# The last batch's Square in two halves about two means, joined by small GpSimd operations

## The reference

```
h   = gelu(x @ W_down[role] + b_down[role])      # 1024 -> 512
u   = h @ W_up[role] + b_up[role]                # 512 -> 1024
y   = x + u
mean = mean(y);  var = mean((y - mean)^2)        # over the 1024 values
out = (y - mean) / sqrt(var + 1e-5) * gamma[role] + beta[role]
```

## Time and profile before

| | us |
|---|---|
| median of 3 runs | 1415.9 |
| lowest, highest | 1415.86, 1416.5 |
| the profiled execution, its own time | 1416.17 |
| its span in the trace | 1414.7 |
| TensorE matmul busy | 1404.9 |
| VectorE busy | 1205.1 |
| ScalarE busy | 776.6 |
| GpSimd busy | 209.8 |

### The profile page before, as it was taken

One profiled execution on the slowest core, in us unless ns is written; L12 is line 12 of the kernel. 1 busy time (PEld: TensorE's weight loads), 2 busy tenths in 40 slices (PEclk: granted clock), 3 DMA queues, 4 the chain that ended last, 5 costly groups with the idle time before them and its releaser, 6 DMA issues.

```text
span 1414.7 us, 29421 instructions
## 1 busy us (share of the span) xinstructions
PE 1404.9 (99%) x6205; PEld 1163.1 (82%) x6206; DVE 1205.1 (85%) x1460; ACT 776.6 (55%) x2049; POOL 209.8 (15%) x312
## 2 busy tenths in 40 slices
PE   9999999999999999999999999999999999999997
PEld 8888888888888888888888888888888888888886
DVE  8798988888888888888899988888888888888887
ACT  5555555555555555555555555555555555555555
POOL 5376411100000000000476311100000000000000
PEclk9999999999999999999999999999999999999999
DMA  9678877766666556666778677766665666666664
GB/s 236 185 228 238 220 205 202 206 207 187 185 198 202 186 185 201 198 187 185 227 233 232 206 213 194 220 188 197 202 187 185 199 200 187 185 196 198 192 187 148
DMA packets 208998, 283.57 MB, mean 200 GB/s; under 512 B 25898, under 2 KB 155691, under 8 KB 208976
## 3 DMA queue, kind: packets, MB, share of 16 engines
q1 hardware_dynamic: 201006, 269.06, 62.5%
q0 software_dynamic: 6016, 12.15, 4.7%
q10 hardware_dynamic: 1954, 2.12, 0.6%
HBM read 183.35 MB, written 99.88 MB: 200 GB/s over the span
## 4 chain that ended last, share of the span: by engine, by line
PE 99%; DVE 1%; issue 0%; DVEq 0%; POOL 0%; POOLq 0%
PE p_up L1168 16%; PE p_up L1170 16%; PE p_up L1169 16%; PE p_down L1168 16%; PE p_down L1170 16%; PE p_down L1169 16%; PE p_down L1144 1%; PE p_down L1216 0%; PE p_down L1211 0%; PE p_down L1222 0%; PE p_up L1211 0%; PE p_up L1222 0%; PE p_up L1216 0%; PE p_hT L1164 0%; DVE row L1108 0%
## 5 line engine op out<-in xcount | busy, mean ns | idle before, releaser
L1168 PE MATMUL p_up<-wu_hi,hT_hi 128*128 x1008 | 392.7, 390 | 0.0
L1170 PE MATMUL p_up<-wu_hi,hT_lo 128*128 x1008 | 392.4, 389 | 0.0
L1169 PE MATMUL p_up<-wu_lo,hT_hi 128*128 x1008 | 392.4, 389 | 0.0
L1168 PE MATMUL p_down<-wd_hi,xT_hi 128*128 x1000 | 389.2, 389 | 0.0
L1169 PE MATMUL p_down<-wd_lo,xT_hi 128*128 x1000 | 389.2, 389 | 0.0
L1170 PE MATMUL p_down<-wd_hi,xT_lo 128*128 x1000 | 389.2, 389 | 0.0
L646 ACT ACTIVATE hT_hi<-p_hT 128x512 fp32r<-128x512 f32 x126 | 75.5, 599 | 382.3 <-DVE p_hT L872 381.2
L892 DVE SCALAR_TENSOR_TENSOR row<-p_up,row 128x1024 f32<-128x1024 f32 x126 | 154.2, 1224 | 126.4 <-PE p_up L1170 126.4
L626 ACT ACTIVATE xT_hi<-xT_raw 128x1024 fp32r<-128x1024 f32 x125 | 132.7, 1062 | 185.9 <-PE p_down L1170 183.4
L1168 PEld LDWEIGHTS p_up<-wu_hi,hT_hi 128*128 128x128 f32 x1008 | 189.2, 188 | 39.6 <-issue 0.7
L1170 PEld LDWEIGHTS p_up<-wu_hi,hT_lo 128*128 128x128 f32 x1008 | 189.4, 188 | 39.4
(11 more groups left out here) (196 smaller groups left out, 1012.1 us busy)
## 6 DMA issues: line engine op xcount, KB each, us to landing
x_quad<-in_x SPq DMA_DIRECT2D x506, 128.0 KB, 3.4
row<-in_x SPq DMA_DIRECT2D x126, 512.0 KB, 4.1
out<-row SPq DMA_DIRECT2D x126, 512.0 KB, 2.8
h_dram<-h SPq DMA_DIRECT2D x125, 256.0 KB, 4.1
h_quad<-h_dram SPq DMA_DIRECT2D x498, 64.0 KB, 2.0
w_raw<-in_L_cond_W_down POOLq DMA_DIRECT2D x64, 64.0 KB, 3.3
w_raw<-in_L_cond_W_up POOLq DMA_DIRECT2D x64, 64.0 KB, 3.7
row<-in_L_cond_W_up SPq DMA_DIRECT2D x16, 128.0 KB, 6.0
```

Of the source, the lines that this page charges most:

```text
L1168: pe.matmul(dst, a_hi, w_hi, start=first, stop=False)
L1169: pe.matmul(dst, a_hi, w_lo, start=False, stop=False)
L1170: return pe.matmul(dst, a_lo, w_hi, start=False, stop=last)
```

## The change

The Square of batch 127 is split. VectorE forms the negative mean of the first 512 columns alone, right behind the first half of the sum; ScalarE then squares these 512 columns about that mean (half_sqsum). When the whole mean is known, ScalarE squares the other 512 columns about the whole mean (sqsum). GpSimd joins both: the variance is half_sqsum / H + 1e-5 + 0.5 * ((sum0 - sum1) / H)^2 + sqsum / H, of which all but the last term is rest_var, in three 128x1 operations; a fourth gives -0.5 * rest_var. ScalarE's Sqrt takes sqsum with rest_var as its bias, and neg_half_var comes by an Identity with bias behind the Sqrt instead of by a Copy ahead of it. last_factor waits for it. A tile of 8 columns is added and the unused tile `spare` is made 8 columns shorter. The branches of ScalarE's body are rewritten so that batch 126 runs the new half Square behind its root.

```diff
--- before.py
+++ after.py
@@ -59,7 +59,7 @@
     PAIRED = LOW + R * NROWS
     FILL = 2 * P
     KEY_TOP = 10 * P - 1
-    SPARE = 32
+    SPARE = 24
     assert FD == FU == RING and HALF == KC and K == 512
 
     with ExitStack() as ctx:
@@ -77,6 +77,8 @@
         ysum = sb("ysum", [P, 2])
         neg_mean = sb("neg_mean", [P, 2])
         sqsum = sb("sqsum", [P, 2])
+        moments = sb("moments", [P, 8])
+        neg_half_mean, half_sqsum, first_var, mean_apart, rest_var, neg_half_rest = (moments[:, n:n + 1] for n in range(6))
         neg_half_var = sb("neg_half_var", [P, 2])
         rstd = [sb(f"rstd{n}", [P, 2]) for n in range(NEWTON + 1)]
         rstd_sq = sb("rstd_sq", [P, 2])
@@ -171,6 +173,9 @@
         squared, scaled, out_ready = sem("squared"), sem("scaled"), sem("out_ready")
         last_half_up, last_step, last_out = sem("last_half_up"), sem("last_step"), sem("last_out")
         last_std_ready, seed_ready, last_plus_bias = sem("last_std_ready"), sem("seed_ready"), sem("last_plus_bias")
+        half_mean_ready, half_squared = sem("half_mean_ready"), sem("half_squared")
+        first_var_ready, mean_apart_ready = sem("first_var_ready"), sem("mean_apart_ready")
+        rest_var_ready, half_rest_ready = sem("rest_var_ready"), sem("half_rest_ready")
         half_var_ready = sem("half_var_ready")
         rstd_ready = [sem(f"rstd_ready{n}") for n in range(NEWTON + 1)]
         square_ready = [sem(f"square_ready{n}") for n in range(NEWTON)]
@@ -571,6 +576,18 @@
                 pool.wait_ge(quad_loaded[b % 2], 16 * NQ * (B // 2) + 16)
                 pool.wait_ge(up_done, b - 1)
                 pool.tensor_tensor(row_of(b, 0), row_of(b, 0), cols(params, at + BU, H), ALU.add).then_inc(last_plus_bias, 1)
+            pool.wait_ge(half_squared, 1)
+            pool.tensor_scalar(first_var[:, :], half_sqsum[:, :], 1.0 / H, LN_EPS, ALU.mult, ALU.add).then_inc(first_var_ready, 1)
+            pool.wait_ge(last_step, 2)
+            pool.tensor_scalar(mean_apart[:, :], last_sum[:, 0:1], last_sum[:, 1:2], 0.5 ** 0.5 / H, ALU.subtract,
+                               ALU.mult).then_inc(mean_apart_ready, 1)
+            pool.wait_ge(first_var_ready, 1)
+            pool.wait_ge(mean_apart_ready, 1)
+            pool.tensor_scalar(rest_var[:, :], mean_apart[:, :], mean_apart[:, :], first_var[:, :], ALU.mult,
+                               ALU.add).then_inc(rest_var_ready, 1)
+            pool.wait_ge(rest_var_ready, 1)
+            pool.tensor_scalar(neg_half_rest[:, :], rest_var[:, :], -0.5, None, ALU.mult).then_inc(half_rest_ready, 1)
+
 
         def first_piece(n):
 
@@ -675,7 +692,11 @@
                 if live(b) and not is_step(i, k, B):
                     round_h(b)
                 b, _, par = seq(i, k, -3)
-                if live(b):
+                if is_last(b):
+                    act.wait_ge(mean_ready, b + 1)
+                    act.activation(p_sq[:, 512:H], row_of(b, 0)[:, 512:H], ACT.Square, bias=neg_mean[:, par:par + 1],
+                                   accum_out=sqsum[:, par:par + 1]).then_inc(squared, 1)
+                elif live(b):
                     act.wait_ge(mean_ready, b + 1)
                     act.activation(p_sq[:, :], row_of(b, turn(i, k, -3)[1]), ACT.Square, bias=neg_mean[:, par:par + 1],
                                    accum_out=sqsum[:, par:par + 1]).then_inc(squared, 1)
@@ -707,19 +728,26 @@
                     act.activation(factor[:, one], rstd_sq[:, one], ACT.Copy, scale=v, bias=1.5).then_inc(factor_ready[0], 1)
                     act.wait_ge(factor_ready[0], b + 1)
                     act.activation(rstd[NEWTON][:, one], r, ACT.Copy, scale=factor[:, one]).then_inc(rstd_ready[NEWTON], 1)
+                if isinstance(b, int) and b == B - 2:
+                    act.wait_ge(half_mean_ready, 1)
+                    act.activation(p_sq[:, 0:512], row_of(B - 1, 0)[:, 0:512], ACT.Square, bias=neg_half_mean[:, :],
+                                   accum_out=half_sqsum[:, :]).then_inc(half_squared, 1)
                 elif is_last(b):
                     v = neg_half_var[:, par:par + 1]
+                    act.wait_ge(seed_ready, 2)
                     act.wait_ge(squared, b + 1)
-                    act.activation(v, sqsum[:, par:par + 1], ACT.Copy, scale=-0.5 / H,
-                                   bias=-0.5 * LN_EPS).then_inc(half_var_ready, 1)
-                    act.wait_ge(half_var_ready, b + 1)
-                    act.activation(last_std[:, :], v, ACT.Sqrt, scale=-2.0).then_inc(last_std_ready, 1)
+                    act.wait_ge(rest_var_ready, 1)
+                    act.activation(last_std[:, :], sqsum[:, par:par + 1], ACT.Sqrt, scale=1.0 / H,
+                                   bias=rest_var[:, :]).then_inc(last_std_ready, 1)
+                    act.wait_ge(half_rest_ready, 1)
+                    act.activation(v, sqsum[:, par:par + 1], ACT.Identity, scale=-0.5 / H,
+                                   bias=neg_half_rest[:, :]).then_inc(half_var_ready, 1)
                     n = number_of(act, b)
                     act.wait_ge(last_out, 2)
                     ring = b % RING
                     act.dma_start(out[bass.ds(n, 1), :, 512:768].rearrange("o t h -> (o t) h"), row[ring][:, 512:768]).then_inc(
                         stored[ring], 16)
-                elif live(b) and not is_step(i, k, B - 1):
+                elif live(b) and not is_step(i, k, B - 1) and not (isinstance(b, int) and b == B - 3):
                     newton(b, par)
 
             act.wait_ge(first_known, 1)
@@ -1094,6 +1122,8 @@
                 dve.scalar_tensor_tensor(before[:, at:at + 512], before[:, at:at + 512], rstd[NEWTON][:, 1 - par:2 - par],
                                          cols(params, at_before + BETA + at, 512), ALU.mult, ALU.add).then_inc(out_ready, 1)
 
+            dve.wait_ge(last_step, 1)
+            dve.tensor_scalar(neg_half_mean[:, :], last_sum[:, 0:1], -2.0 / H, None, ALU.mult).then_inc(half_mean_ready, 1)
             write_before(0)
             dve.wait_ge(up_done, b + 2)
             dve.scalar_tensor_tensor(y[:, 512:H], p_up[par][:, 512:H], 1.0, y[:, 512:H], ALU.mult, ALU.add,
@@ -1120,6 +1150,7 @@
             dve.wait_ge(last_std_ready, 3)
             dve.reciprocal(last_seed[:, :], last_std[:, :]).then_inc(last_step, 1)
             dve.wait_ge(last_step, 3)
+            dve.wait_ge(half_var_ready, b + 1)
             dve.tensor_scalar(last_factor[:, :], last_seed[:, :], last_seed[:, :], neg_half_var[:, par:par + 1], ALU.mult,
                               ALU.mult).then_inc(last_step, 1)
             dve.wait_ge(last_step, 4)
```

## The result

The change made the kernel slower: 1419.18 us (1418.96 to 1419.63, 16 runs) against 1416.19 us (1415.8 to 1416.67, 16 runs) before, 2.99 us more, a ratio of 1.0021 with a 95% interval of 1.0015 to 1.0028. The forecast was 1416.3, at most 1417.1. The profiled execution has a span of 1417.4 us where it had 1414.7.

A forecast was written before the change was run, and what follows sets the result against it. The prediction took VectorE's queue behind the last matmul as the bound. It summed +0.31 (VectorE operation), +0.10 (GpSimd's reads) and 0 (ScalarE savings) to +0.4 us on a median of 1415.9, forecasting 1416.3, range 1415.5 to 1417.1.

The forecast's parts named there:

- The bound: Tail behind the last matmul: VectorE's own queue, without a hole from 1405.66, sets the end; reciprocal follows the scaling.
- forecast slack on ScalarE: ScalarE's tail chain: the 0.55 us saved by the shorter Square and dropped Copy become slack, VectorE being later.
- Sqrt over well before the second scaling ends: Sign of a right forecast in the tail: ScalarE's Sqrt ends at 1408.79, reciprocal due at 1409.55.
- (1): ScalarE's last Square on 512 columns instead of 1024: 0.72 instead of 1.12 us, 0.40 saved on ScalarE.
- (3): First half's Square added on ScalarE behind batch 126's newton: 0.84 us, hidden by a gap of 1.9 us.
- (2): ScalarE: Copy leaves the way to the Sqrt, net 0.15 us saved; Sqrt with bias 0.29, Identity another 0.29.
- Rival B: Slower: ScalarE's Identity needs another table load of 1.28 us, +1.1, giving 1417.0; chance 0.04.
- (4): One small VectorE operation more between first sum and batch 126's write moves all behind it by 0.31 us (0.18 to 0.35).
- (5): Four small GpSimd operations in the tail, nothing queued behind them; inputs ready in time, reads cost VectorE 0.1 us (0 to 0.57).
- rival A: Slower: GpSimd's rest_var passed over twice, getting in only after both scalings; last_factor +1.15 us, giving 1417.05; chance 0.10.
- D: Something outside the tail moves, in the long TensorE-bound stage, by up to 1 us either way; chance 0.05.

The follow-up runs named there:

- drain_first: Changed kernel with bounded waits plus one more GpSimd DRAIN ahead of its four small operations: 1416.97 us against 1416.28 for the kernel before, ratio 1.0005.
- late_drain_after_loads: Kernel before with bounded waits, a late GpSimd addition nobody waits for, and a GpSimd DRAIN behind the loading phase: 1416.34 us against 1416.2, ratio 1.0001.
- control_after: Changed kernel with register maxima added on VectorE and TensorE that bound the waited-for values: 1419.12 us against 1415.99 for the kernel before, ratio 1.0022.
- drain_first_shifted: Changed kernel with bounded waits, an early additional GpSimd DRAIN and three unused VectorE memsets: 1417.1 us against 1416.2 for the kernel before, ratio 1.0007.

## Why the prediction was wrong

- **The bound: right up to the reciprocal, its margin wrong.** VectorE's queue sets the start of the reciprocal; halving the Square and dropping the Copy brought nothing. The reciprocal stands directly behind the scalings in every kernel here; in the changed one it is 3.72 behind the last matmul's start, where 3.40 + 0.31 was forecast. But the forecast slack on ScalarE did not come: the Sqrt was to be over at 1408.79 and was over at 1409.30, 0.21 ahead of the second scaling's end, where the kernel before had 0.30. The named sign "Sqrt over well before the second scaling ends" was not met. The hand-over from ScalarE to VectorE took 0.11 here (neg_half_var's end at 1409.91 to last_factor at 1410.02), so the Sqrt was only some 0.02 from holding the reciprocal. The 0.04 by which the prediction counted 0.18 us to spare is the hand-over in the other direction; with 0.11 it is 0.11.
- **(1), (3): right.** The half Square took 0.69 (0.72 forecast), and the added one (1405.85 to 1406.66) is hidden.
- **(2): right in its prices** (Sqrt and Identity with bias 0.29 each), and no third table load: the changed kernel has two, as before, the later one at 1392.4. Rival B fell.
- **(4): right.** 0.31 forecast, 0.32 measured, 0.31 alone.
- **(5): this step failed, and in two ways.** First, "it has nothing queued behind them". The block's own DRAIN is queued behind them, and the description of the kernel before has the same fault where it says that GpSimd has nothing left to do behind L573. It is in the trace of before, 10.05 us long and hidden, on GpSimd's queue, where no view of busy engines counts it; I had read the queues of VectorE and ScalarE to their ends and not that of GpSimd. It is 2.1 of the 2.8 us. The rule that I applied to ScalarE's wait, who is queued behind it, I did not apply past the last line of the source.
- Second, GpSimd's reads. I priced them at 0.1 on VectorE, by delayed VectorE operations. On VectorE they cost nothing that can be seen: its writes and scalings keep their spacing of 0.67. The price fell on GpSimd itself: 0.39 us of the 2.8. rest_var was issued at 1407.81 beside a write that ended at 1408.18, did not get in there but behind the next operation, and so the fourth operation ended at 1409.59 instead of 1409.1 and last_factor was 0.40 late. That is rival A's mechanism at one boundary instead of two; I had seen this case ("Identity by 1409.2 or, if neg_half_rest is late by another boundary, 1410.0") and let it cost nothing, although 1410.0 is behind the 1409.74 at which last_factor was due.
- **The Trainium skill**, SBUF — State Buffer, section Who interferes with whom, has the loser of that port wait for the whole instruction of the other; the rows agree (0.69 for an operation of 0.19, ended 0.05 behind the write). The prediction's reading of it, by which up to 0.5 would fall on VectorE, did not come true: GpSimd was the one that waited each time.
- **The chances.** 0.02 for slower came from the cases that I had priced, all of which ended within the tail. The end of the kernel is a meeting of five queues; a case for "another queue ends last" was missing, and D, with "nothing speaks for it", was no substitute.

## What to carry to other kernels

An engine that is idle at the end is not free there: its DRAIN at the block's end comes behind whatever is moved into the tail, and here GpSimd's ended 7.6 us behind it. Look up each engine's DRAIN in the trace, its start and its length, before giving an idle engine late work; if it is long and late work must go ahead of it, try a DRAIN of one's own where that engine idles (drain_first, late_drain_after_loads). And a small GpSimd operation beside back-to-back VectorE operations of 0.75 us with two SBUF inputs took 0.53 to 1.09 us here, not its own 0.19. And the margin of the input that is second latest counts too: here the work that joins the two halves used up what the shorter Square had freed.

## What was not expected of the hardware

- GpSimd's DRAIN ended 7.6 us behind its last operation (1387.1, 1408.4, 1408.7, 1409.6 and 1409.7 in five kernels), once only: the DRAIN took 0.4 at 27 us and 7.6 at 921 us, and ended 0.1 behind the last operation in the three kernels where it followed such a DRAIN.
- GpSimd's operation gets in between two back-to-back VectorE operations, but not always at the first boundary. Started 0.36 us ahead of the next VectorE start it got in there (control_after, 1408.79 against 1409.15; drain_first alike), started 0.29 ahead it did not (the changed kernel, 1407.81 against 1408.10; drain_first_shifted alike). Why is open.
- VectorE stood still for 0.34 at one place of its instruction stream with no wait, and with three more instructions ahead of it the gap was gone from the tail. A hold-up of the same 0.41 on its queue is hidden behind the second write in the kernel before. That it is the fetching of instructions is a guess: no run here shows it.
